# A graph network in one kernel: ranking edges with sums on TensorE, and eight PSUM banks in the convolutions' second product

## The chip, the cores and the metric

The kernel runs on one core of a Trainium2 chip. Its engines work in parallel, each through a list of its own: TensorE (PE) multiplies matrices, VectorE (DVE) and ScalarE (ACT) work element by element, GpSimd (POOL) and the sync engine (SP) mostly start transfers. They wait for each other by semaphores. The metric is the device time of one execution in microseconds; lower is better. PSUM, where PE writes, has eight banks of 512 f32 columns.

## The reference

A graph of 3125 nodes with 256 features and 50,000 edges, sorted by target, passes through four layers. Each adds to x what a graph operation makes of the normalised x:

```python
edge_index = jnp.stack([src, dst])
h = jnp.maximum(_layernorm(x, axis=-1), 0.0)
x = x + _L0_gnn_ref(h, src, dst, ...)      # two attention convolutions, 4 heads
h = jnp.maximum(_layernorm(x, axis=-1), 0.0)
x = x + _L1_gnn_ref(h, edge_index, edge_attr_128, node_vec1, node_vec1_n2, ...)
h = jnp.maximum(_layernorm(x, axis=-1), 0.0)
x = x + _L2_gnn_ref(h, weight, src, dst, edge_type_8, edge_weight)   # relations
h = jnp.maximum(_layernorm(x, axis=-1), 0.0)
x = x + _L3_gnn_ref(h, edge_index, edge_weight, ...)   # two convolutions
```

Two pieces matter here. The second layer sums each edge's 128 attributes over the edge's *source*, while the edges are sorted by target:

```python
sum3d = jax.ops.segment_sum(edge_attr @ W_sum + b_sum, src, num_segments=num_nodes)
cent_term = jax.nn.sigmoid(centralities @ W_cent + b_cent)
vor_term = jax.nn.sigmoid(voronoi_values @ W_vor + b_vor)
```

and the last layer runs this twice:

```python
h = jax.nn.relu(x @ w1 + b1)
agg = jax.ops.segment_sum(ew[:, None] * h[src], dst, num_segments=x.shape[0])
h = agg @ w2 + b2
return jax.nn.relu(_bn(h, g, b))           # statistics over all nodes
```

## The kernel before, in words

Nodes are cut into NT = 25 tiles of 128, edges into two halves of 196 columns of 128. The program has three blocks: one for the setup and the two attention convolutions, one for the middle layers, one for the relations and the last two convolutions (`tail`).

**Sorting the attributes.** In each attention convolution one half of the edge attributes is put in order of the source. DVE works out each edge's place (`rank_half`, one call a half): it marks for every edge and every node tile whether the edge's source lies in that tile (L518), takes running counts over 25 x 196 = 4900 columns (L521), lets PE make prefix sums over the partitions (`rank_prefix`, three small matmuls), adds the tile's offset to the running count and multiplies by the mark, tile by tile (L540, 25 instructions), and sums over the 25 tiles to one place per edge (L543). POOL then writes the rows to their places in DRAM with 196 indirect transfers (the scatters, L509), 128 edges each. SP loads the rows to be scattered into two buffers of seven columns; each is loaded again when its seven scatters are through.

**Setup, engine by engine.** PE makes 25 encoder products, one a node tile: four rows times 512 columns (L1155). Behind the sixteenth, in PE's list, stands the first half's `rank_prefix`. Then come eight transposes of the edges' low index bits (L1164, DVE copies them out at L1133), the projection of the 25 tiles (`pe_project`, L718 and L728, with the second half's `rank_prefix` inside) and the small matmuls for the step tables. ACT takes the sigmoid of each encoder product, POOL adds its two halves and SP stores the sum; in POOL's list the 25 additions stand ahead of the scatters, so the scatters wait for all of them and for the places. DVE does, in order: the first half's places, the edges' integer parts, the eight copies, the row statistics of x (`first_norm`, L565 to L574, in whose middle it waits for ACT's square root), the fold of the attention vectors, the second half's places, the masks (`make_masks`, L807), and the step tables, of which the last instruction is L670.

**The look.** For every edge the scores of its two ends are looked up: 98 groups of four edge columns, in a loop over four groups. A group is 24 matmuls (L910), one-hot vectors from ACT and DVE, a product with the masks (L877) and a sum (L886) on DVE. Softmax follows, then the aggregation. POOL starts the aggregation's gathers (L153) as soon as its scatters are done and the tables are there, and stops after 56 of them, when its ring of 28 slots is full, until the aggregation takes slots out.

**The tail's convolution** (`pe_convolve`, `act_convolve`, `dve_convolve`). The aggregated features, 25 tiles by 256 columns, are turned on PE (two 128x128 transposes a tile, L1606) into one of two PSUM banks, copied out to SBUF a tile at a time, even tiles by ACT and odd ones by DVE (L1615), and multiplied with the second weight in chunks of four tiles (512 columns, L1596) into two other banks, which ACT evicts (L1623) and DVE takes statistics of (L1648). In PE's list the four tiles of the next chunk are turned ahead of the current chunk's product. Four of the eight banks stand idle in this stretch. The batch statistics need all nodes, so all that follows waits for the last chunk.

## Time and profile before

| | us |
|---|---|
| time, median of 3 runs | 4706.84 |
| lowest and highest | 4700.74 and 4716.11 |
| the profiled execution's own time | 4672.72 |
| its span (first to last instruction) | 4671.0 |
| PE busy | 2342.8 (50%) |
| POOL busy | 2384.8 (51%) |
| DVE busy | 2088.9 (45%) |
| ACT busy | 1410.8 (30%) |
| mean granted TensorE clock | 0.711 |

No engine is busy much over half the time, so the shares don't say what bounds the kernel: the stages have different limits, and the timeline of each stage has to be read. The granted clock is a share of 2.4 GHz; in the records PE runs at either 1.2 or 2.4 GHz. A matmul of f32 appears in the trace as two records.

### The profile page before, as it was taken

The numbers are of one execution on the slowest core, as the hardware profiler recorded it, in microseconds if no ns is written. First come the engines' busy times: TensorE is split into PE (matmuls) and PEld (weight loads), VectorE is DVE, ScalarE is ACT, GpSimd is POOL, SyncE is SP. The second block draws the span as 40 slices with busy tenths as digits, with TensorE's granted clock in tenths as the row PEclk, the third lists the DMA queues.
The fourth block names the chain that finished last, engine by engine and source line by source line (L and its number), as shares of the span: only waits on it lengthen the run. The fifth ranks groups of instructions, "written<-read, shape, count | busy, mean of one in ns | idle before, by whom it ended". The sixth has DMA issues, their size and how long they took to land. (4 is left out here: it accounts for less than half of the span.)

```text
span 4671.0 us, 63853 instructions
## 1 busy us (share of the span) xinstructions
PE 2342.8 (50%) x11271; PEld 1694.6 (36%) x11272; DVE 2088.9 (45%) x5444; ACT 1410.8 (30%) x4653; POOL 2384.8 (51%) x2446
## 2 busy tenths in 40 slices
PE   5301646566441246465655834555635556445556
PEld 2201534444330135344444313333423334234334
DVE  6501984445340169654445813333423334233336
ACT  2100746666540146466666710000200001200002
POOL 4775005556637520355552555666366663566660
PEclk9655977777665579677777966666756668666667
DMA  3443433333224334333332842333233331323331
GB/s 111 124 108 91 128 112 91 100 104 104 79 71 119 109 111 127 93 102 101 104 89 74 257 154 83 91 91 92 72 90 91 91 91 37 98 85 91 91 91 40
DMA packets 339578, 465.58 MB, mean 100 GB/s; under 512 B 108191, under 2 KB 253928, under 8 KB 336112
## 3 DMA queue, kind: packets, MB, share of 16 engines
q0 software_dynamic: 113824, 289.70, 21.6%
q1 hardware_dynamic: 157536, 109.12, 8.2%
q10 hardware_dynamic: 67956, 64.45, 4.9%
q14 instruction: 242, 1.98, 0.1%
q8 instruction: 20, 0.33, 0.0%
HBM read 385.88 MB, written 76.97 MB: 99 GB/s over the span
## 5 line engine op out<-in xcount | busy, mean ns | idle before, releaser
L301 PE MATMUL t_ps<-t_ring,t_hot 128*128 x2640 | 884.3, 499 | 893.9 <-DVE t_hot L212 447.7
L153 POOL DMA_INDIRECT ring<-feat_d,srcC x784 | 755.2, 963 | 1060.6 <-ACTq L167 821.2
L301 PEld LDWEIGHTS t_ps<-t_ring,t_hot 128*128 128x128 f32 x2640 | 637.9, 252 | 1140.8 <-issue 1028.7
L153 POOL DMA_INDIRECT t_ring<-feat_d,srcC x784 | 742.2, 947 | 488.0 <-issue 217.6
L175 ACT ACTIVATE ring<-ring,exC 128x64 f32<-128x64 f32 x3136 | 813.4, 336 | 112.1 <-issue 111.0
L301 PE MATMUL bank<-ring,arena 128*128 x1760 | 642.5, 500 | 96.0 <-ACT ring L175 42.9
L910 PE MATMUL wide<-arena 128*128 128x100 bf16 x4704 | 276.9, 217 | 462.7 <-issue 289.4
L509 POOL DMA_INDIRECT attr_d<-abuf,attr_pos x392 | 405.3, 1034 | 191.2 <-issue 129.2
L228 DVE TENSOR_TENSOR acc<-acc,t_ps 128x256 f32 x440 | 184.3, 419 | 712.5 <-DMA arena<-in_L_gnn_ar 223.7
L153 POOL DMA_INDIRECT t_ring<-rel_d,relC x392 | 371.2, 947 | 221.2 <-issue 113.0
L301 PEld LDWEIGHTS bank<-ring,arena 128*128 128x128 f32 x1760 | 400.4, 252 | 174.4 <-issue 120.2
L212 DVE TENSOR_SCALAR t_hot<-lane,dlocT,weightT 128x128 f32<-128x128 f32 x1320 | 412.9, 358 | 94.9 <-issue 63.0
L291 PE MATMUL wide<-arena 128*128 x880 | 243.2, 368 | 410.1 <-DVE arena L220 289.8
L910 PEld LDWEIGHTS wide<-arena 128*128 128x128 bf16 x4704 | 239.8, 102 | 500.2 <-issue 307.7
L291 PEld LDWEIGHTS wide<-arena 128*128 128x128 f32 x880 | 207.3, 255 | 519.7 <-issue 486.3
L1615 ACT COPY t_ring<-t_pt 128x256 f32<-128x256 f32 x26 | 9.6, 369 | 1192.7 <-PE t_pt L1606 1192.7
L877 DVE TENSOR_TENSOR arena<-wide,masks 128x800 f32<-128x800 f32 x196 | 191.9, 979 | 324.7 <-remote 228.8
L228 DVE TENSOR_TENSOR acc<-acc,bank 128x261 f32 x440 | 187.7, 427 | 216.4 <-issue 110.2
L228 DVE TENSOR_TENSOR X<-X,t_ps 128x256 f32 x220 | 92.0, 418 | 348.6 <-DMA X<-in_x 213.7
L206 DVE TENSOR_TENSOR arena<-lane,dlocT 128x256 f32<-128x256 f32 x440 | 185.4, 421 | 121.3 <-issue 107.5
L829 ACT ACTIVATE arena<-arena,ones 128x512 bf16<-128x512 bf16 x196 | 141.4, 722 | 304.7 <-remote 219.9
L234 DVE TENSOR_TENSOR acc_a<-acc_a,wide 128x129 f32 x440 | 127.5, 290 | 200.2 <-issue 129.2
(274 smaller groups left out, 2246.9 us busy)
## 6 DMA issues: line engine op xcount, KB each, us to landing
arena<-lo_d ACTq DMA_DIRECT2D x392, 128.0 KB
rel_d<-mid_stage SPq DMA_DIRECT2D x25, 1024.0 KB
arena<-attr_d SPq DMA_DIRECT2D x98, 260.0 KB
abuf<-in_attr SPq DMA_DIRECT2D x56, 448.0 KB
ring<-feat_d,srcC POOLq DMA_INDIRECT x784
t_ring<-feat_d,srcC POOLq DMA_INDIRECT x784
feat_d<-arena ACTq DMA_DIRECT2D x50, 128.0 KB
feat_d<-t_stage SPq DMA_DIRECT2D x50, 128.0 KB, 1.7
```

Source lines behind the costliest of these rows:

```text
L153: pool.indirect_dma_start(out=ring[:, u % RING, j, 0:D], out_offset=None, in_=table, in_offset=bass.IndirectOffsetOnAxis(ap=index[:, u, j: ...
L175: last = act.activation(part_of_row, part_of_row, ACT.Copy, scale=exC[:, bass.ds(u, 1), j, h])
L206: last = dve.tensor_tensor(hot[:, k % NHOT, :, :], lane[:, :].unsqueeze(1).to_broadcast([P, 2, P]), dlocT[:, bass.ds(s, 1), :].rearrange(" ...
L212: last = dve.tensor_scalar(hot[:, k % NHOT, j, :], lane[:, :], dlocT[:, bass.ds(s, 1), j], weightT[:, bass.ds(s, 1), j], ALU.is_equal, ALU ...
L228: dve.tensor_tensor(acc[:, tile, 0:g.width], acc[:, tile, 0:g.width], ps[k % NHOT][:, 0:g.width], ALU.add).then_inc(g.added, 1)
L234: dve.tensor_tensor(acc_a[:, tile, :], acc_a[:, tile, :], ps_a[k % NHOT][:, 0:AW - 1], ALU.add).then_inc(g.attr_added, 1)
L291: pe.matmul(ps_a[k % NHOT][:, 0:AW - 1], hot_a[:, k % NHOT, :], aring[:, slot, 0:AW - 1], start=True, stop=True).then_inc(g.attr_done, 1)
L301: last = pe.matmul(ps[k % NHOT][:, 0:g.width], hot[:, k % NHOT, j, :], ring[:, slot, j, 0:g.width], start=(j == 0), stop=(j == 1))
L509: pool.indirect_dma_start(out=attr_d, in_=abuf[:, g % 2, k, :], in_offset=None, out_offset=bass.IndirectOffsetOnAxis(ap=attr_pos[:, at + k ...
L829: act.activation(looked[:, k % 2, 1, :], apart[:, k % 2, :], ACT.Relu, scale=-1.0, bias=ones[:, 0:1]).then_inc(s_dst_hot[l], 1)
L877: dve.tensor_tensor(cand[:, k % 2, :, :, :], pk[k % 2][:, :, :].rearrange("p b (s x) -> p (b s) x", x=P)[:, :, 0:HEADS * NT] .rearrange("p ...
L910: last = pe.matmul(pk[k % 2][:, j // 2, at:at + HEADS * NT], looked[:, k % 2, q, j * P:(j + 1) * P], tab[:, piece, q * HEADS * NT:(q + 1) ...
```

## The change

Setup:

- PE's first `rank_prefix` moves ahead of the encoder products. 
- `rank_half` loses its sum over the tiles (L543). The 25 tile products are instead summed by 25 matmuls with the identity into one PSUM bank, `sum_places`. For the first half two of them stand ahead of each encoder product, until all are done ahead of the thirteenth; for the second half all 25 follow the projection.
- The conversion of the sums to places becomes a function of its own, `place_half`. DVE does the row statistics ahead of it in the first half, and the masks ahead of it in the second.
- The eight transposes stand behind encoder product 18, and wait for the first half's places, since both use the same bank. The fold of the attention vectors stands ahead of the wait for the square roots, which is now `first_roots`.
- The sigmoid results have six buffers instead of three. SP loads the attribute groups 2 and 3 ahead of the stores of the low bits.

Tail: tiles are turned in pairs, four transposes into one full bank, over four banks, and copied out a pair at a time; the chunk products use four banks too. The evictions and statistics of chunk r-2 stand ahead of the copies of chunk r's pairs.

```diff
+    NSIG = 6
+    p_pos = wide[0][:, 0, 0:HC]
...
         for n in range(NT):
             dve.scalar_tensor_tensor(out=running[:, n, :], in0=running[:, n, :], scalar=offset[:, n:n + 1],
-                                     in1=mk[:, n, :], op0=ALU.add, op1=ALU.mult)
-        dve.drain()
-        dve.reduce_sum(pos[:, :], running.rearrange("p n j -> p j n"), AX.X)
-        dve.drain()
-        dve.tensor_copy(pos_i[:, 0, :], pos[:, :])
+                                     in1=mk[:, n, :], op0=ALU.add, op1=ALU.mult).then_inc(s_placed, 1)
+        dve.drain()
+
+    def place_half(dve, h):
+        at = h * HC
+        dve.wait_ge(s_ranked, h + 1)
+        dve.tensor_copy(pos_i[:, 0, :], p_pos)
...
+    def sum_places(pe, h, first, last):
+        for n in range(first, min(last, NT)):
+            pe.wait_ge(s_placed, NT * h + n + 1)
+            done = pe.matmul(p_pos, ident[:, :], running[:, n, :], start=(n == 0), stop=(n == NT - 1))
+            if n == NT - 1:
+                done.then_inc(s_ranked, 1)
...
         @block.sync
+            for g in range(2, 4):
+                stage_attr(sp, g)
             for q in range(2):
                 for c in range(4):
                     sp.wait_ge(s_loc, 4 * q + c + 1)
                     sp.dma_start(lo_d[q, c * QC:(c + 1) * QC, :], loT[0:QC, 4 * q + c, :]).then_inc(s_low, 16)
-            sp_weights(sp, 0, 2)
+            sp_weights(sp, 0, 4)
...
         @block.vector
+            first_norm(dve)
+            place_half(dve, 0)
             for n in range(8):
                 dve.wait_ge(s_lot, n + 1)
                 dve.tensor_copy(loT[0:QC, n, :], p_lo[n % 2][0:QC, 0:P]).then_inc(s_loc, 1)
-            first_norm(dve)
             fold_attention(dve, 0)
+            first_roots(dve)
             rank_half(dve, 1)
+            make_masks(dve)
+            place_half(dve, 1)
             dve.sem_inc(s_acol, 1)
-            make_masks(dve)
             step_tables(dve)
...
         @block.tensor
+            pe.wait_ge(s_ready, 1)
+            rank_prefix(pe, 0)
             pe.wait_ge(s_enc_in, 16 * 8)
             for n in range(NT):
+                sum_places(pe, 0, 2 * n, 2 * n + 2)
                 wait_from(pe, s_sig, n - 1)
                 pe.matmul(banks[n % 2][:, :], enc_l[:, n * P:(n + 1) * P], enc_r, start=True, stop=True)\
                   .then_inc(s_enc, 1)
-                if n == 15:
-                    pe.wait_ge(s_ready, 1)
-                    rank_prefix(pe, 0)
+                if n == 18:
+                    pe.wait_ge(s_int, 1)
+                    pe.wait_ge(s_pos, 1)
...
             pe_project(pe, 0)
+            pe.wait_ge(s_loc, 8)
+            sum_places(pe, 1, 0, NT)
...
         def pe_convolve(pe, z):
+            def turn_pair(q):
+                a0, a1 = PAIR[q]
+                if q >= 4:
+                    pe.wait_ge((s_ata, s_atd)[q % 2][z], (q - 4) // 2 + 1)
+                for n in range(a0, a1):
+                    for c in range(KD):
+                        at = c * 2 * P + (n - a0) * P
+                        last = pe.transpose(p_turn[q % 4][:, at:at + P], acc[:, n, c * P:(c + 1) * P], ident[:, :])
+                last.then_inc(s_at[z], 1)
             def chunk(r):
-                    if r:
-                        pe.wait_ge(s_g[z], KD * (r - 1) + c + 1)
+                    if r >= 2:
+                        pe.wait_ge(s_g[z], KD * (r - 2) + c + 1)
                     for a in range(KD):
-                        last = pe.matmul(pf[c][:, 0:(a1 - a0) * P], W2[:, z, a, c * P:(c + 1) * P],
+                        last = pe.matmul(p_proj[(KD * r + c) % 4][:, 0:(a1 - a0) * P], W2[:, z, a, c * P:(c + 1) * P],
                                          AT[:, a, a0 * P:a1 * P], start=(a == 0), stop=(a == KD - 1))
+            for r in range(NR + 1):
+                for q in range(2 * r, min(2 * r + 2, NQ)):
+                    turn_pair(q)
                 if r:
                     chunk(r - 1)
...
         def act_convolve(act, z):
+            for r in range(NR + 1):
+                if r >= 2:
+                    evict(r - 2)
+                if 2 * r < NQ:
+                    copy_turned(act, act.copy, z, 2 * r)
```

PE's list from the start of the setup, before (`wide` are the banks of the ranking and of the low bits, `ring` holds the running counts, `masks` the encoder's input; L1155 is the encoder product, L557 to L559 the prefix sums, L1164 the transposes, L718 the projection's turn):

```order
L1155 MATMUL bank<-masks 128x512 x16
L557 MATMUL wide<-total,before 128x25
L558 MATMUL wide<-total,ones 128x25
L559 MATMUL wide<-ones,total 25x1
L1155 MATMUL bank<-masks 128x512 x9
L1164 MATMUL wide<-ident,exC 98x128 x8
L718 MATMUL bank<-ident,arena 128x128 x4
```

The same stretch of PE's list in the changed kernel (L569 is the sum of the places, L1177 the encoder product, L1185 the transposes; the dots stand for ten more rounds of the two):

```order
L562 MATMUL wide<-total,before 128x25
L563 MATMUL wide<-total,ones 128x25
L564 MATMUL wide<-ones,total 25x1
L569 MATMUL wide<-ring,ident 128x196 x2
L1177 MATMUL bank<-masks 128x512
...
L569 MATMUL wide<-ring,ident 128x196
L1177 MATMUL bank<-masks 128x512 x7
L1185 MATMUL wide<-ident,exC 98x128 x8
L1177 MATMUL bank<-masks 128x512 x6
L732 MATMUL bank<-ident,arena 128x128 x4
```

The prefix sums moved from behind sixteen encoder products to the front, 25 sums came in between the first thirteen, and the transposes moved ahead of the last six.

DVE's list from the first half's tile products on, before:

```order
L540 SCALAR_TENSOR_TENSOR ring<-ring,offset 128x196 x25
L543 TENSOR_REDUCE masks<-ring 128x196
...
L552 SCALAR_TENSOR_TENSOR attr_pos<-masks 128x196
...
L1133 CAST ring<-wide 98x128 x8
L565 BN_STATS stats<-ring 128x6 x25
...
L518 TENSOR_TENSOR ring<-tile_no,hi_f 128x4900
```

The same of the changed kernel:

```order
L543 SCALAR_TENSOR_TENSOR ring<-ring,offset 128x196 x25
...
L577 BN_STATS stats<-ring 128x6 x25
...
L557 SCALAR_TENSOR_TENSOR attr_pos<-ring 128x196
L1151 CAST ring<-wide 98x128 x8
...
L521 TENSOR_TENSOR ring<-tile_no,hi_f 128x4900
```

The reduction is gone, and the row statistics stand ahead of the places.

PE's list in a tail convolution, before, with the bank numbers (L1606 is the turn of a tile, L1596 the product):

```order
L1596 MATMUL t_pf0<-t_ring,t_w2 128x512 x2
L1596 MATMUL t_pf1<-t_ring,t_w2 128x512 x2
L1606 MATMUL t_pt0<-ident,acc 128x128 x2
L1606 MATMUL t_pt1<-ident,acc 128x128 x2
L1606 MATMUL t_pt0<-ident,acc 128x128 x2
L1606 MATMUL t_pt1<-ident,acc 128x128 x2
```

The same of the changed kernel (L1620 the turn, L1631 the product):

```order
L1631 MATMUL t_pf0<-t_ring,t_w2 128x512 x2
L1631 MATMUL t_pf1<-t_ring,t_w2 128x512 x2
L1620 MATMUL t_pt0<-ident,acc 128x128 x4
L1620 MATMUL t_pt1<-ident,acc 128x128 x4
L1631 MATMUL t_ps2<-t_ring,t_w2 128x512 x2
L1631 MATMUL t_ps3<-t_ring,t_w2 128x512 x2
L1620 MATMUL t_ps0<-ident,acc 128x128 x4
L1620 MATMUL t_ps1<-ident,acc 128x128 x4
```

A bank of the turns now comes back after four pairs instead of after one other tile.

## Rows read from the trace of the kernel before

**Rows 1.** Timeline of DVE, setup: start us, duration us, engine, line, operation, [idle before].

```profile
55.87 0.15 DVE L528 COPY col_f<-wide 25x1 f32<-25x1 f32 x1 [32.08 <-PE wide L559]
57.00 11.35 DVE L540 SCALAR_TENSOR_TENSOR ring<-ring,offset 128x196 f32<-128x196 f32 x25
68.42 8.83 DVE L543 TENSOR_REDUCE masks<-ring 128x196 f32<-128x4900 f32 x1
...
85.76 8.25 DVE L565 BATCH_NORM_STATS2 stats<-ring 128x6 f32<-128x256 f32 x25
...
103.21 5.26 DVE L518 TENSOR_TENSOR ring<-tile_no,hi_f 128x4900 bf16<-128x4900 f32 x1 [0.75 <-issue]
108.55 10.37 DVE L521 TENSOR_TENSOR_SCAN ring<-ones,ring 128x4900 f32<-128x4900 f32 x1
...
187.71 0.62 DVE L670 CAST relC<-bank 128x196 int32<-128x196 f32 x2
```

**Rows 2.** Timeline of PE, setup.

```profile
27.01 27.67 PE L1155 MATMUL bank<-masks 4*128 4x512 f32 x32 [27.01 <-DMA masks<-in_L_gnn_b_vor]
...
80.42 0.66 PE L1164 MATMUL wide<-ident,exC 128*98 128x128 f32 x2 [8.93 <-DVE exC L1121]
...
84.85 0.66 PE L1164 MATMUL wide<-ident,exC 128*98 128x128 f32 x2 [0.17 <-DVE ring L1133]
...
104.33 2.13 PE L728 MATMUL bank<-arena 128*128 128x264 f32 x4
...
109.61 1.15 PE L728 MATMUL bank<-arena 128*128 128x264 f32 x4
```

**Rows 3.** Timeline of POOL, setup.

```profile
72.20 0.73 POOL L1069 TENSOR_TENSOR arena<-arena 128x256 f32<-128x256 f32 x1 [0.98 <-ACT arena L1088]
80.05 1.35 POOL L509 DMA_INDIRECT attr_d<-abuf,attr_pos  x1 [7.13 <-issue]
...
109.62 10.07 POOL L509 DMA_INDIRECT attr_d<-abuf,attr_pos  x1 [0.30 <-issue]
...
355.66 0.97 POOL L509 DMA_INDIRECT attr_d<-abuf,attr_pos  x1 [0.30 <-issue]
...
426.15 0.95 POOL L153 DMA_INDIRECT ring<-feat_d,srcC  x1 [0.30 <-issue]
```

**Rows 4.** Timeline of DVE, first look.

```profile
370.65 0.99 DVE L877 TENSOR_TENSOR arena<-wide,masks 128x800 f32<-128x800 f32 x1 [65.15 <-remote]
...
436.45 0.99 DVE L877 TENSOR_TENSOR arena<-wide,masks 128x800 f32<-128x800 f32 x1 [63.66 <-remote]
```

**Rows 5.** Timeline of PE, first look, then the second layer's.

```profile
416.73 0.24 PE L910 MATMUL wide<-arena 128*128 128x100 bf16 x1 [2.56 <-issue]
...
453.13 0.91 PE L910 MATMUL wide<-arena 128*128 128x100 bf16 x9 [0.46 <-issue]
...
1680.59 1.16 PE L910 MATMUL wide<-arena 128*128 128x100 bf16 x12 [0.46 <-issue]
```

**Rows 6.** Timeline of POOL, second layer's look: its last gather before it waits.

```profile
1671.27 0.95 POOL L153 DMA_INDIRECT ring<-feat_d,srcC  x1 [0.30 <-issue]
```

**Rows 7.** Windows: stretch, length, busy of PE, PEld, DVE, ACT, POOL (xcount), clock, DMA.

```profile
250.00:300.00 50.00, 2.90 (x12) 1.16 (x11) 0.00 (x0) 0.00 (x0) 36.98 (x39) 0.50 0.43 106
...
500.00:600.00 100.00, 61.00 (x1163) 54.84 (x1164) 100.00 (x146) 70.27 (x98) 0.00 (x0) 0.98 0.46 128
```

**Rows 8.** Timeline of PE, first tail convolution.

```profile
3930.02 0.66 PE L1606 MATMUL t_pt<-ident,acc 128*128 128x128 f32 x4 [1.04 <-DVE acc L228]
...
3933.38 3.60 PE L1596 MATMUL t_pf<-t_ring,t_w 128*128 128x512 f32 x8
...
3939.08 3.60 PE L1596 MATMUL t_pf<-t_ring,t_w 128*128 128x512 f32 x8
...
3959.63 0.38 PE L1606 MATMUL t_pt<-ident,acc 128*128 128x128 f32 x2
...
3964.22 0.71 PE L1596 MATMUL t_pf<-t_ring,t_w 128*128 128x128 f32 x4 [0.33 <-ACT t_ring L1623]
```

85 lines of the change are left out of this document (37 added, 48 removed).

## The prediction

> **What bounds the kernel now.** I first read busy time in slices: no engine is full, so the question is asked stage by stage. The changed stages are the setup (first 190 us) and the two tail convolutions (35 us each). For each I read the timelines of PE, DVE and POOL side by side, then the windows further on, to see what the stage hands over.
>
> In the setup DVE has the longest list: it waits 32.08 us for the prefix sums, which stand behind sixteen encoder products on PE [rows 1, 2], and its last table instruction ends at 188.3 [rows 1]. The natural reading is that a shorter DVE list shortens the kernel. The look that follows says otherwise. While POOL issues indirect transfers one behind the other, the look crawls: from 250 to 300 us PE gets through 12 matmul records and DVE through none; from 500 to 600 DVE does 146 instructions, three a group, so a group takes 2.05 us [rows 7]. In the crawl a group takes 436.45 - 370.65 = 65.8 us [rows 4]. POOL's last gather ends at 427.1 [rows 3], and from 453.1 PE runs at full pace [rows 5]. The second layer repeats it: last gather ends at 1672.2 [rows 6], full pace from 1680.6 [rows 5]. So nearly all of the 98 groups wait for POOL to stop, and setup time is passed on only through that moment. Whatever slows PE there (the rows call its gaps "issue") I take as found.
>
> POOL's stop is its scatters' start plus a block of fixed length: 80.05 to 427.1, 347 us for 196 scatters and 56 gathers [rows 3]. The tables (188.3) are ready 168 us before the gathers need them (scatters end at 356.6). And the start waits for two things: the last encoder addition, which ended at 72.93, and the places, which came 7.1 us later [rows 3]. After the change I must ask which is late.
>
> In the tail convolution PE is the bound: a chunk begins every 5.70 us (3933.38, then 3939.08), of which 8 product records take about 3.4 us (3.60 with the last one's latency) and the rest is four turned tiles with waits for the copies out of two banks [rows 8].
>
> **The encoder stretch, part by part.** Prefix sums first: they are out about 25 us, as soon as DVE's totals are (it stops at 23.8 = 55.87 - 32.08), so the 25 tile products start about 26.5 instead of 57.0 and, at their 11.35 us, end about 38 [rows 1]. The integer parts and the row statistics (8.25 us and some 4 of small work) follow and end about 54; they now fill what was a wait. DVE's 8.83 us sum is gone twice.
>
> On PE the first half gains 25 sums. No row shows a 128x128 by 196-column f32 product, so I bound it by the nearest: four records of 264 columns took 2.13 us at the low level, thus 1.07 a product, times 196/264 = 0.79 us; at the high level 1.15, thus 0.43 [rows 2]. Less than nothing is excluded, since PE has to do them. The encoder products take 27.67/16 = 1.73 us each [rows 2]. That is the low clock: 0.865 a record of 512 columns, where the tail's records of that size take 0.43 to 0.45 (3.60/8) [rows 8]. I take 0.72 a sum, between its scaling from the 264-column row and from the encoder's record (0.865 x 196/512 x 2 = 0.66): 18 us. The eight transposes with their copies (80.42 to 85.5, [rows 2]) now stand inside the encoder's list, and add about 4.7 us. So the products end at 27.0 + 25 x 1.73 + 18 + 4.7 = 93 us, where they ended about 71.4, and the last addition 1.5 us later, at 94.5. The places are ready long before: the sums end at 27.5 + 12 x 1.73 + 18 = 66.3 and DVE's five small steps take 2.8 (77.25 to 80.05, [rows 1, 3]): 69. What is late next is the encoder: the scatters start at 94.3, **14 us later** than before. Behind the additions on POOL's list stand just these scatters. ACT's square root too waits behind the last sigmoid (about 93.5); DVE's second half starts near 96 instead of 103.2.
>
> **The rest of the setup.** The second half loses its 8.83 us sum (25 sums on PE lie beside the masks), so the tables end about 7 + 9 = 16 us earlier, at 172. No gather waits for them, so this is worth only an earlier first group of the look; a quarter of a group, 0.5 us. More sigmoid buffers: worth nothing, since ACT waited for PE, not for the stores. SP's attribute loads ahead of the low-bit stores: each waits for seven scatters, which delays the stores to about 130, and the look wants them at 175; nothing. POOL's block stays 347 us: its long issue of 10.07 us lies under DVE's 10.37 us scan [rows 1, 3], and the second half's mark and scan still fall within the scatters (96 to 112). The Trainium skill, "SBUF - State Buffer", section on the "DVE blocks DMA" trap, says that GpSimd can't write descriptors while certain DVE instructions hold the shared port. By that rule the hold goes where the scan goes; the trace agrees (10.07 beside 10.37), and had the scatters started first at 112 the block would be about 19 us shorter.
>
> **When the look gets free.** POOL stops at 427.1 + 14 = 441. The lag to full pace was 26.0 us in the first look and 8.4 in the second [rows 3, 5, 6]. I read the difference as position in the 65.8 us group: the first stop fell into the gap between two groups (PE's last crawling matmul at 416.73 [rows 5], the group ended by 436.45 [rows 4]), in which nothing could speed up; the second fell behind a group's beginning. After the change the group boundaries lie 16 us earlier (354.6, 420.4) and the stop at 441, in the middle of a group's matmuls, so I expect 12 us of lag, from between 8.4 and 26: full pace at 453, which is where it was, with as many groups done. **Setup: 14 later, 14 less lag: 0**, with -4 and +12 as the lag's ends.
>
> **The tail.** The chunk stays 3.43 us; a turned tile back to back costs 0.22 us (3959.63 to the product of the next chunk, whose two records end it in 0.22 to 0.38 [rows 8]), so four cost 0.9 and a period is 4.33 instead of 5.70: 1.37 saved in each of the four full periods, 5.5 us. At the start 16 records with waits took 3.36 us (3930.02 to 3933.38); back to back, and the last pair's copy, 2.0: 1.35 saved. At the end the last chunk waited 0.33 us for an eviction; now it doesn't. Sum 7.2 us a convolution, **14.4 for two**. Cover: ACT per period then has two evictions and a 512-column copy, about 2.0 us, DVE the same, beside 4.33 on PE; a pair is copied one whole chunk before it is needed. If the turns cost twice that (the bounds are 0.22 and 0.38 a tile) the saving is 5 a convolution. The batch statistics wait for the last chunk, so all of it reaches the end.
>
> **Sum.** Profiled execution 4672.7, less 14.4, plus 0: 4658. It stands 34 us below the median of the runs; carried over to that: 4706.8 - 14.4 = **4692 us**. About 0.3%, 14 us, is what a measurement here can tell from none, so this forecast lies on the edge of it.
>
> **Rivals.**
> 1. *The lag stays 26 us* wherever the stop falls. For: it may belong to the first look, not to the position. Against: 8.4 in the other. Then the 14 us late start counts in full: 4692 + 14 = 4706.
> 2. *The sums lift PE's clock.* The encoder products alone ran 45 us at the low level with PE full [rows 2]; the sums are 128-row products like those behind which it rose after 104. With sums and products high the thirteen rounds take 13 x 0.87 + 25 x 0.36 = 20 us, twelve lone products again 1.73: scatters from 76, 4 us earlier than before, and the lag short: setup -20, total 4672. Against: the sums fill less than half of the stretch. The Trainium skill, "TensorE: Matmul & The Clock Gate", Part 1, has the gate opened by sustained busy time; by that alone the encoder stretch would have run high already, which the trace contradicts (1.73 us, not 0.87). By the page it would come out as this rival, or better.
> 3. *Slower: the stop falls into the head of the gap between two groups.* The gap is about 20 us (416.73 to 437, [rows 4, 5]); behind it PE needed 16 more. If the boundaries don't shift as I think and the stop comes at the gap's start, the lag is 36: setup +14 +10 = +24, total 4692 + 24 = 4716, slower than before. It decides from a lag of 27 us on.
> 4. *The look isn't held by POOL's stop*, and DVE's 16 us come through: 4692 - 16 = 4676. Against: rows 7. For: only that I can't name what slows PE.
>
> **Chances.** Forecast 0.40, rival 1 0.20, rival 2 0.13, rival 3 0.15, rival 4 0.08; the remaining 0.04 is something unseen. The forecast's cloud (4685 to 4700) is split between faster and same. Faster 0.24 + 0.02 + 0.13 + 0.08 = 0.47, slower 0.09 of rival 3 plus 0.03 and 0.02 of the rest = 0.14, same 0.39. Range 4668 (rival 2) to 4720 (rival 3); the forecast's own is 4684 to 4704.
>
> **What the changed profile would show.** Encoder products in rounds of about 3.2 us and the last addition near 94; scatters from 94 (76 in rival 2). Product records of 0.43 us in that stretch would refute the low clock. Last gather at 441, tables at 172, the lag read between them and the first full-pace group, of 12 (26 in rival 1, 36 in rival 3). In the tail, chunks every 4.33 us and 27.7 us from first turn to last eviction. The forecast is wrong if scatters don't start later, or if the look reaches full pace before POOL stops.

## The result

| | before | after |
|---|---|---|
| median of 20 runs, us | 4706.84 | 4715.72 |
| lowest and highest | 4690.56 to 4721.62 | 4706.78 to 4726.79 |
| the profiled execution's own time | 4672.72 | 4715.71 |
| its span | 4671.0 | 4713.2 |

The ratio is 1.0018, 95% interval 1.0010 to 1.0027: the change makes the kernel slower by 5 to 13 us. The forecast was 4692 us, with 0.47 on faster, 0.39 on the same and 0.14 on slower. The two profiled executions differ by 43 us, the medians by 9: the profiled execution of before was 34 us shorter than its median, and shorter than every one of its twenty runs. So differences are read here stage by stage, and not from the spans.

### The profile page after: what moved, and what is told of

Same layout as the page of the kernel before. It is cut to its first block and busy times, and to the rows that moved or that the text cites. A ratio compares the mean times of both kernels' runs of the same rounds, so it can differ in the third digit from the quotient of the medians.

```text
span 4713.2 us, 64027 instructions
## 1 busy us (share of the span) xinstructions
PE 2379.8 (50%) x11371; PEld 1726.8 (37%) x11372; DVE 2065.1 (44%) x5430; ACT 1410.2 (30%) x4641; POOL 2398.7 (51%) x2446
## 5 line engine op out<-in xcount | busy, mean ns | idle before, releaser
L301 PE MATMUL t_ps<-t_ring,t_hot 128*128 x2640 | 888.2, 502 | 902.1 <-DVE t_hot L212 456.1
L220 DVE TENSOR_SCALAR arena<-lane,arena,minus_tile 128x128 f32<-128x128 f32 x440 | 159.1, 362 | 145.1 <-issue 81.8
```

The source lines that it names most:

```text
L220: dve.tensor_scalar(hot_a[:, k % NHOT, :], lane[:, :], aring[:, slot, AW - 1:AW], minus_tile[:, g.attr, bass.ds(s, 1)], ALU.subtract, ALU. ...
L301: last = pe.matmul(ps[k % NHOT][:, 0:g.width], hot[:, k % NHOT, j, :], ring[:, slot, j, 0:g.width], start=(j == 0), stop=(j == 1))
```

## The profile after

The page of the changed kernel, its first rows:

```profile
span 4713.2 us, 64027 instructions
PE 2379.8 (50%) x11371; PEld 1726.8 (37%) x11372; DVE 2065.1 (44%) x5430; ACT 1410.2 (30%) x4641; POOL 2398.7 (51%) x2446
```

PE's timeline in the setup answers to [rows 2] (start, duration, engine, line, operation, idle before and its releaser):

```profile
23.53 0.59 PE L562 MATMUL wide<-total,before 128*128 128x25 f32 x2 [23.53 <-DVE offset L529]
...
28.04 2.07 PE L1177 MATMUL bank<-masks 4*128 4x512 f32 x2
30.04 1.68 PE L569 MATMUL wide<-ring,ident 128*128 128x196 f32 x4
31.64 2.07 PE L1177 MATMUL bank<-masks 4*128 4x512 f32 x2
...
70.66 12.31 PE L1177 MATMUL bank<-masks 4*128 4x512 f32 x14
82.90 0.67 PE L1185 MATMUL wide<-ident,exC 128*98 128x128 f32 x2
...
86.01 10.60 PE L1177 MATMUL bank<-masks 4*128 4x512 f32 x12
```

A round of two sums and a product takes 31.64 - 28.04 = 3.60 us. Behind the last sum a product takes 1.76 again (12.31/7), and the eight transposes with their copies 3.1 (82.90 to 86.01). The list ends at 96.6.

POOL's timeline answers to [rows 3]: the last addition, the first scatter, and the last gather before its wait.

```profile
97.32 0.72 POOL L1085 TENSOR_TENSOR arena<-arena 128x256 f32<-128x256 f32 x1 [0.98 <-ACT arena L1104]
98.22 1.16 POOL L512 DMA_INDIRECT attr_d<-abuf,attr_pos  x1 [0.17 <-issue]
...
446.37 0.95 POOL L153 DMA_INDIRECT ring<-feat_d,srcC  x1 [0.30 <-issue]
```

The first scatter is 18.2 us later than before (80.05), and POOL stops at 447.3 instead of 427.1, so its block is 349.1 us long, 347 before.

DVE's timeline of the first look, answering to [rows 4]: one product with the masks a group.

```profile
365.61 0.99 DVE L891 TENSOR_TENSOR arena<-wide,masks 128x800 f32<-128x800 f32 x1 [65.30 <-issue]
432.33 0.99 DVE L891 TENSOR_TENSOR arena<-wide,masks 128x800 f32<-128x800 f32 x1 [64.58 <-remote]
473.80 0.99 DVE L891 TENSOR_TENSOR arena<-wide,masks 128x800 f32<-128x800 f32 x1 [39.19 <-PE wide L924]
475.86 0.98 DVE L891 TENSOR_TENSOR arena<-wide,masks 128x800 f32<-128x800 f32 x1
```

Full pace begins at 473.80, 26.5 us behind POOL's stop. In the kernel before, the same count gave 453.48 - 427.1 = 26.4. So the look, too, is 20 us later, and ends at 666.0 instead of 645.6.

PE's timeline of the first tail convolution, answering to [rows 8]:

```profile
3983.30 1.09 PE L1620 MATMUL t_pt<-ident,acc 128*128 128x128 f32 x8 [0.65 <-DVE acc L228]
...
3989.65 3.60 PE L1631 MATMUL t_ps<-t_ring,t_w 128*128 128x512 f32 x8
3993.09 1.04 PE L1620 MATMUL t_ps<-ident,acc 128*128 128x128 f32 x8
3993.96 3.60 PE L1631 MATMUL t_pf<-t_ring,t_w 128*128 128x512 f32 x8
...
4009.67 1.05 PE L1631 MATMUL t_pf<-t_ring,t_w 128*128 128x128 f32 x8
```

A chunk every 4.31 us (5.70 before), and 27.4 us from the first turn to the end of the last product record (34.9 before); the second convolution is the same, 27.4.

Between these stages the two profiles drift further apart: the changed kernel is 20 us behind at the first look's full pace, 30 at the second's (1710.83 against 1680.88, by DVE's products) and 53 at the tail's first turn (3983.30 against 3930.02). Most of that lies in the execution of before, not in the change: from the second look's full pace to the first turn it took 2249 us, where the five profiled kernels with the new tail (the changed one and four of the experiments, on chips on which before takes about 4705 us) took 2266 to 2278.

Setup +20, tail -15: this already names the direction. The experiments had to show whether these two do add up, why the encoder's list became so long, and what the first scatter's time is worth.

## The experiments

They fell on several chips, and this turned out to matter. On four of them the kernel before takes 3535 to 3537 us, on one 4703, like the chip of the forecast. Every run is compared with the kernel before on its own chip. I call the four the A chips, and that one and the forecast's the B chips (in the expectations the two are "conditions"). One window tells them apart, 250 to 300 us, in the first look (busy time and count of each engine, granted clock, DMA share, GB/s), first the changed kernel on the B chip:

```profile
250.00:300.00 50.00, 2.95 (x17) 1.46 (x17) 1.84 (x3) 0.72 (x1) 36.90 (x39) 0.50 0.43 106
```

and the setup-only kernel on an A chip:

```profile
250.00:300.00 50.00, 30.91 (x576) 27.76 (x576) 50.00 (x72) 34.31 (x49) 33.24 (x35) 0.97 0.83 217
```

POOL issues its scatters at much the same pace (39 and 35), but on the A chip PE does 576 matmul records beside them, on the B chip 17. There the crawl doesn't exist, and the look takes 2.1 us a group from its first.

**1. The two halves of the change.** `setup_only` is the changed kernel with the tail functions of before; `tail_only` the reverse. Edit: the change's own hunks, all of the setup or all of the tail.

> The change's setup alone, with the tail of before. Theory T (the setup counts only through the moment at which POOL stops issuing its scatters and gathers, and that moment goes by the encoder's last addition plus a fixed block of 347 to 349 us): first scatter at about 98, stop at about 447, the look at full pace at about 475, the two convolutions at 34.9 us each as in before; +20 us, so a ratio of 1.004 (4727 against 4707). Rival A (the setup costs nothing that the median shows, and the stages behind it are slower by themselves): first scatter at 98 too, but a ratio of 1.000 to 1.002. Rival B (the whole of the +9 us comes from the tail's code): ratio of 1.000.

> The change's tail alone, with the setup of before. Theory T: first scatter at 80, stop at 427, look at full pace at 453, each convolution 27.4 us instead of 34.9; -15 us, a ratio of 0.9968. Rival A (the stages behind the setup are slower by themselves): -15 us too, and the setup-only kernel tells. Rival B (the eight banks cost more elsewhere than they give): ratio of 1.000 or more.

Measured, both on an A chip: setup_only 1.0057 (1.0043 to 1.0071), +20 us; tail_only 0.9957 (0.9943 to 0.9971), -16 by the medians. The sum is +4. Rivals A and B fall. The halves were not run by themselves on a B chip. But the reason I gave for the setup can't be right on this chip, where no look waits for POOL's stop. What takes its place is seen in POOL's waits. On the A chip (setup_only, from 395 to 900 us; line waited for, us in total, times, longest):

```profile
POOL ring L153 <- issue: 107.6, 353, 0.3
POOL ring L153 <- ACTq L167: 11.6, 38, 0.3
```

and on the B chip (the changed kernel, 447 to 1290 us):

```profile
POOL ring L153 <- ACTq L167: 425.1, 71, 268.2
```

On the A chip POOL never waits for a free slot of the first layer's ring longer than 0.3 us. From its first scatter to the end of the next layer's scatters it goes through its list with short waits only: 26 of them, 35 us in all, are for the rows that SP loads (3.1 us at most), and none of any kind is over 4.4 us. So its own list is the bound there, and a delay of its first scatter is passed on one for one; that this holds for the total too is what the table behind the experiments tests. (The chain of waits on that page can't show it: the 31% that POOL has in it are all gathers of later layers, into `t_ring`.)

On the B chip the same 19 us come through another gate, POOL's stop and the look behind it. I call the joint form T2: what counts of the setup is the first scatter.

**2. The sums on DVE again.** `prefix_reduce` keeps the early prefix sums, the six buffers and the new tail. DVE sums over the tiles again, and converts the first half's sums to places right behind them, ahead of the integer parts and the row statistics.

```
 in rank_half / place_half:
-            ... .then_inc(s_placed, 1)
+        dve.reduce_sum(pos, running.rearrange("p n j -> p j n"), AX.X)
 on PE:
-                sum_places(pe, 0, 2 * n, 2 * n + 2)
-                if n == 18: (the eight transposes)
+            (the eight transposes behind the encoder's loop)
-            sum_places(pe, 1, 0, NT)
```

> The changed kernel, but the sums over the 25 tiles go back to DVE as one reduction, right behind the tile products, and the transposes go back behind the encoder products; the prefix sums stay first, the sigmoids keep six buffers, the tail is the changed one. Theory T with the PE list as the cause of the late additions: the encoder products stand at 2.0 to 2.2 us each again, the last addition at 72 to 80, first scatter at 72 to 80, stop at 419 to 427, full pace at 445 to 453; with the tail's -15 us the ratio to before is 0.995 to 0.997. Rival (position theory: the lag from POOL's stop to full pace depends on where in a group of the look the stop falls): the same stop, but full pace off by up to 14 us either way. Rival (the six buffers or POOL and ACT themselves make the additions late, not PE's list): first scatter stays at 95 or later, ratio 1.002.

Measured: 0.9942 (0.9928 to 0.9955), and on another A chip (below, `prefix_again`) 0.9923 (0.9910 to 0.9937), both under the 0.995 to 0.997 that I expected, which was reckoned for a B chip. First scatter at 71.8, as expected. The encoder on PE is one row now:

```profile
27.16 43.03 PE L1177 MATMUL bank<-masks 4*128 4x512 f32 x50 [2.02 <-DMA masks<-in_L_gnn_b_vor]
```

25 products in 43.0 us, 1.72 each, and DVE, which has nothing to wait for, has the places at 46.4. PE's list made the additions late, not the six buffers, which this kernel has too.

**3. Gathers behind the look.** Edit: `pool.wait_ge(s_sum[l], LOOKS + 2)` ahead of each layer's gathers.

> The changed kernel with one more wait in each attention layer: POOL starts its first 56 gathers when the look is over, instead of right behind the scatters. Theory T (the look crawls at 65 us a group of four edge columns while POOL issues indirect transfers back to back, and reaches 2.05 us a group some 25 us after it stops): layer 1 stops at 374 instead of 447, full pace at about 400 instead of 475, look over at about 590 instead of 666; in layer 2 the look starts at full pace from its first group, some 60 us earlier; the gathers then fit into the softmax, which takes 49 us; in all -110 to -140 us against the changed kernel, ratio to before about 0.972. Rival (the crawl comes from something else that ends at 450 to 475, such as the transfers' landing, the clock, or the scores' table): full pace stays at 450 to 475 and the gathers behind the look add 20 to 70 us to each layer, ratio 1.01 to 1.03. Rival (the aggregation now starts late, since its first slots are filled only in the softmax, and softmax crawls while POOL issues): the look gains as T says but the softmax grows by as much, ratio 1.00.

> The kernel gathers_wait once more, for the condition in which before takes about 4705 us. There, theory T (POOL's back-to-back indirect transfers make the look crawl, and it reaches full pace 26 us after they end): scatters over at 374, nothing behind them until the look is done; full pace at 400 instead of 474, look over at 592 instead of 666, in layer 2 the look at full pace from its first groups; -110 to -150 us against the changed kernel, ratio to before 0.970 to 0.980. Rival (the look's pace depends on something else that ends at 450 to 475): full pace at 450 to 475, ratio 1.01 or more. Rival (the gain of the look is given back by gathers that now fall into the softmax and slow it): look over at 592, aggregation no more than 20 us earlier, ratio 0.995 to 1.002. In the other condition (before at 3535): as measured, 1.009.

> As for gathers_wait_again: with before at about 4705, theory T has full pace at 400, the look over at 592 and -110 to -150 us against the changed kernel (ratio to before 0.970 to 0.980); the rival with another cause of the crawl has full pace at 450 to 475 and a ratio of 1.01 or more; the rival in which the gathers' crawl moves into the softmax has the look over at 592 and a ratio of 0.995 to 1.002. With before at about 3535: 1.009 as measured twice.

Measured on three A chips: 1.0093, 1.0096 and 1.0079 (intervals within 1.0058 to 1.0112). There the scatters end at 393.7 and the look at 389.2, so the first layer has no wait, while in the second POOL stands from 1172.4 to 1206.7, 34 us. POOL's list being the bound, most of that comes out: 26 or 27 us against the changed kernel. It was made to tell whether the look of a B chip is released by the end of the scatters or by the stop of POOL, but it never ran on one. So that POOL's transfers hold the look there stays a reading of the timelines, and no run shows it by removing them.

**4. The changed kernel on an A chip, and its transposes and sums moved.** `transposes_late` puts the eight transposes behind the encoder's loop again; `sums_behind` the 25 sums too, ahead of them.

```
 sums_behind:
             for n in range(NT):
-                sum_places(pe, 0, 2 * n, 2 * n + 2)
                 ... (the encoder product)
+            sum_places(pe, 0, 0, NT)
+            (the eight transposes)
```

> The changed kernel, unchanged. In the four kernels run so far the kernel before took 3535 us, not 4707, and its look ran at 2.1 us a group from the start instead of 65; POOL waited nearly nowhere. Theory T2 (in this condition POOL's list of scatters and gathers is the bound from its first scatter on, so that every us by which the first scatter moves comes out at the end, one for one): first scatter at 98 to 99 against 80, +19 to +20, the tail -15; ratio 1.0010 to 1.0020. Rival (the effects of setup, +20, and tail, -15, don't add up): a ratio under 1.000 or over 1.003. Should this run meet the other condition (before at about 4707): 1.0018, the profile as seen before.

> The changed kernel with the eight transposes of the low bits back behind the last encoder product; the places' sums stay between the products. Theory T2: PE's encoder list gets 3 us shorter, the last addition goes from 97 to 94, first scatter at 95, -3 us at the end against the changed kernel (ratio to before about 1.0005). Rival (the transposes stood in a gap of PE's and cost nothing): first scatter stays at 98.

> The changed kernel with all 25 sums of the first half's places behind the last encoder product (and the transposes behind them). Theory T2: the products stand at 1.71 us each, the last one ends at 70, the additions at 72; then 25 sums of 0.8 us (no product between them) end at 90, and the places are there at 92 to 93; first scatter at 93, -5 to -6 us against the changed kernel (ratio about 0.9998). Rival (the sums are dear only between products, for the clock or for the bank): the sums take 0.4 us each when they stand alone, first scatter at 82 to 83, ratio about 0.997. Rival (a wait that is not PE's): first scatter stays at 98.

Measured: after_again 1.0020 (1.0011 to 1.0029), first scatter at 98.1; transposes_late 1.0012 (1.0002 to 1.0023), at 95.6; sums_behind 0.9976 (0.9965 to 0.9988), at 83.7. The change has the same price on both kinds of chip, 1.0018 and 1.0020. Without the transposes in PE's list the first scatter comes 2.5 us earlier, and the medians differ by 2 us (3 expected). The sums alone were not 0.8 us each, as I expected, but as the rival had it, 0.44:

```profile
70.01 11.08 PE L569 MATMUL wide<-ring,ident 128*128 128x196 f32 x50
```

The windows of these records alone (66 to 81 us) show why; the first column behind the length is PE's busy time and count.

```profile
66.00:70.00 4.00, 0.00 (x0) 0.00 (x0) 1.00 0.18 66
70.00:74.00 4.00, 3.99 (x12) 3.99 (x13) 1.00 0.18 66
74.00:78.00 4.00, 4.00 (x22) 4.00 (x22) 1.00 0.01 4
78.00:81.00 3.00, 3.00 (x19) 2.79 (x17) 1.00 0.00 0
```

Twelve records in 4 us are 0.33 each, the pace of 1.2 GHz; nineteen in 3 us are 0.16, that of 2.4. (The granted clock's column reads 1.00 in all of these, also where a record has the length of 1.2 GHz, so I go by the durations here.) Behind 43 us of four-row products PE stood at the low level; 128-row products in a row lifted it, and mixed with four-row ones, as in the changed kernel, they didn't. So 26.5 us of longer list (96.6 against 70.1) are 11.1 for the sums by themselves, 3.1 for the transposes, and 12 for mixing the sums with the products; 9 of the 12 are the sums (0.80 us each instead of 0.44) and 3 to 4 the products between them (2.00 instead of 1.72).

**5. Two other mixtures.** `sums_first` has the 25 sums ahead of the encoder's loop; `five_a_round` has `sum_places(pe, 0, 5 * n, 5 * n + 5)` in it.

> The changed kernel with all 25 sums of the first half's places ahead of the first encoder product (the transposes stay behind product 18). Theory T2 with the pace of PE as it was seen: sums at 26.4 to about 37 (they follow DVE's tile products, which end at 34.7), then products at 0.865 us a record again although the sums stood before them, the last at 83, first scatter at 84 to 85, so -13 to -14 us against the changed kernel, ratio to before about 0.998. Rival (128-row sums bring PE to its high pace and the four-row products keep it): products at 0.43 us a record, additions limited by ACT and POOL, first scatter at 62 to 68, ratio 0.992 to 0.994. Rival (it is only the amount of PE's work, not the alternation, that counts): the list ends at 96, first scatter stays at 98, ratio 1.002.

> The changed kernel with five sums ahead of each of the first five encoder products instead of two ahead of each of the first thirteen; nothing else is moved. A round of two sums and a product took 3.60 us: 1.71 for the product as it stands alone, 2 x 0.67 for the sums at PE's low pace, and 0.55 that is left for the change from one to the other. Theory T2 with a price per change: 8 rounds fewer, -4.4 us, first scatter at 93 to 94, ratio 1.0007. Rival (the extra is per sum): first scatter stays at 98, ratio 1.002. Rival (five sums in a row, 2 to 3 us, are enough to raise PE's pace): sums at 0.33 to 0.44 us, first scatter at 88 to 91, ratio 0.999 to 1.000.

Both ran on the B chip. Measured: sums_first 0.9973 (0.9958 to 0.9989), first scatter at 82.0; five_a_round 0.9976 (0.9958 to 0.9995), at 81.6. PE's rows in five_a_round:

```profile
27.03 3.63 PE L569 MATMUL wide<-ring,ident 128*128 128x196 f32 x10 [1.90 <-DMA masks<-in_L_gnn_b_vor]
30.60 2.07 PE L1177 MATMUL bank<-masks 4*128 4x512 f32 x2
...
37.44 1.93 PE L569 MATMUL wide<-ring,ident 128*128 128x196 f32 x10
39.30 1.12 PE L1177 MATMUL bank<-masks 4*128 4x512 f32 x2
...
45.13 21.25 PE L1177 MATMUL bank<-masks 4*128 4x512 f32 x30
```

My price per change of kind (0.55 us) is refuted: the first scatter comes 12 us earlier than that gave. The third rival was nearer (88 to 91 for the 81.6 measured): from the third round on five sums take 1.93 us, not 3.63, and the product between them 1.12, not 2.07; both at the high level. sums_first came out 2 to 3 us earlier than expected (84 to 85), since its products don't fall to the low level at once. The products' own windows, first just behind the sums, then further on:

```profile
37.40:41.00 3.60, 3.60 (x8) 1.23 (x9) 1.00 0.05 16
41.00:66.00 25.00, 25.00 (x31) 9.12 (x30) 0.51 0.24 87
```

Eight records of 0.45 us, then 0.81 at a granted clock of 0.51, which is 1.2 GHz: the four-row products don't keep the level that the sums won. The Trainium skill, "TensorE: Matmul & The Clock Gate", Part 1, ties the level to how busy PE has been. The trace doesn't agree with that alone: PE was full from 41 to 66 and fell, and full before 70 in sums_behind and didn't rise. What differed was the kind of product, four rows or 128. The number of columns doesn't explain it: the tail's products have 512 columns as well, but 128 rows, and run at 0.43 us a record (3.60/8 with the end of the last one).

**6. The additions on DVE.** `adds_dve` is prefix_reduce with POOL's 25 additions put into DVE's list, among the places, integer parts and row statistics. Two things had to move with them: SP loads three groups of attributes amid and right behind the stores of the encoder's sums, and DVE folds the attention vectors ahead of its eight copies. `first_and_dve` in addition takes the first half's places from PE, with the sums ahead of the encoder.

```
-            for n in range(NT):                       (POOL)
-                pool.wait_ge(s_sig, n + 1)
-                pool.tensor_tensor(sigb[...], ..., ALU.add).then_inc(s_term, 1)
+    def add_halves(dve, first, last):                 (DVE, called from seven places of its list)
+        for n in range(first, last):
+            dve.wait_ge(s_sig, n + 1)
+            dve.tensor_tensor(sigb[...], ..., ALU.add).then_inc(s_term, 1)
```

> prefix_reduce with the 25 additions of the encoder's halves on DVE, between its other work, instead of on POOL, so that POOL's first scatter waits for the places alone; two loads of scatter groups are issued amid the stores of the encoder's sums. Theory T2: places and first scatter at 46 to 48 instead of 71.8, scatters over at about 340, 56 gathers at about 412; DVE's list is 8 us longer, so look, softmax and the start of the aggregation's additions come 6 to 10 us later, at 429 to 433, and POOL, which has filled its ring, now waits for them: of the 25 us only 2 to 8 come out at the end, ratio about 0.992 to 0.994. Rival (POOL's list is the bound whatever comes: all 25 us come out): ratio 0.987. Rival (the look's later start costs more than the scatters' earlier one gives): ratio 0.995 or more. Should the run meet the other condition (before at 4707): stop of POOL at 412 instead of 419 to 427 and more, the look at full pace some 25 us after it, ratio 0.992.

> adds_dve once more. With before at about 4705: first scatter at 47.8, stop at 398 to 399, full pace at 424, so 32 us earlier than before, and the tail's 15: ratio 0.990, which is 0.001 above first_and_dve's 0.9887 in that condition, since there POOL's block alone counts. With before at about 3535: 0.988 as measured, under first_and_dve's 0.989.

> adds_dve with the first half's places summed on PE ahead of the encoder instead of by DVE's reduction: first scatter at 39 to 41 instead of 47.8. The encoder's products start 10 us later, so look, softmax and the aggregation's first addition come 8 to 12 us later, at 434 to 438. Theory T2 with its limit (POOL's list is the bound only as long as the aggregation starts by the time at which POOL's 56 gathers are through, which adds_dve reached with a first wait of 6.7 us): no gain, +2 to +10 us against adds_dve, ratio 0.988 to 0.991. Rival (POOL's list alone counts): -8 us, ratio 0.9855.

> first_and_dve once more, for the condition in which before takes about 3535 us. There, T2 with its limit: first scatter at 41 against 47.8 of adds_dve, but the aggregation's first addition at 434 to 438 against 426, POOL waits for it 10 to 20 us, total not under adds_dve's: ratio 0.988 to 0.991. Rival (POOL's list alone counts): 0.986. In the other condition (before at 4705): as measured, 0.989.

Measured on A chips: adds_dve 0.9877 (0.9856 to 0.9899) and 0.9860 (0.9839 to 0.9881), first_and_dve 0.9891 (0.9876 to 0.9906); on the B chip first_and_dve 0.9887 (0.9867 to 0.9908). With adds_dve I had counted on POOL's waiting for a later look and on 2 to 8 of 25 us to come out (0.992 to 0.994). The first scatter came 24 us earlier, and 21 and 23 us of that came out, as the rival had it. Its longest wait was this:

```profile
418.88 0.95 POOL L153 DMA_INDIRECT ring<-feat_d,srcC  x1 [0.30 <-issue]
426.49 0.94 POOL L153 DMA_INDIRECT ring<-feat_d,srcC  x1 [6.67 <-ACTq L167]
```

The look began at 170.7, not later than prefix_reduce's 169.1, and the aggregation's first addition came at 426.3, 3 us later instead of 6 to 10. One step on, the limit is there; first_and_dve, whose first scatter stands at 40.4:

```profile
405.77 1.55 POOL L153 DMA_INDIRECT ring<-feat_d,srcC  x1 [0.30 <-issue]
432.27 0.95 POOL L153 DMA_INDIRECT ring<-feat_d,srcC  x1 [24.95 <-ACTq L167]
```

POOL has filled its ring at 407.3 and stands for 25 us until the aggregation starts. The 7 us by which its scatters start earlier are lost, and the kernel takes 9 to 12 us more than adds_dve. On A chips adds_dve is the fastest kernel of this study, 1.2 to 1.4% under the one before. It did not run on a B chip, so whether it or first_and_dve is faster there is open.

**7. More work ahead of the look.** `masks_twice` is prefix_reduce with `make_masks(dve)` a second time, some 22 us more on DVE and nothing on POOL; `prefix_again` is its partner.

> prefix_reduce with the masks made twice on DVE, 22 us more of DVE's work ahead of the look and none on POOL's list. Theory T2 with its limit: first scatter stays at 72, the look and the aggregation's first addition come 22 us later, at 445; POOL's 56 gathers are through at about 437, so 8 to 14 us of the 22 come out, ratio 0.9965 to 0.998. Rival (only POOL's first scatter counts): ratio 0.994. Rival (the look is the bound after all): all 22 us come out, ratio 1.0005.

> masks_twice once more, for the condition in which before takes about 3535 us. There, T2 with its limit: first scatter at 72, the aggregation's first addition at 445 against 423 of prefix_reduce, of the 22 us 8 to 14 come out: ratio 0.9965 to 0.998 (prefix_reduce: 0.9942). Rival (only the first scatter counts): 0.994. Rival (the look is the bound): 1.0005. In the other condition (before at 4705): equal to prefix_again within 0.15%, since the 22 us lie ahead of a look that crawls until POOL's stop.

> prefix_reduce once more, as the partner of masks_twice. In the condition with before at 4705: first scatter at 72, stop at 422 to 424, full pace at 448 to 450, ratio 0.995 to 0.996. In the other (before at 3535): as measured, 0.994.

Measured on one A chip: masks_twice 0.9945 (0.9932 to 0.9959), prefix_again 0.9923 (0.9910 to 0.9937). The first scatter is the same (71.3 and 71.9) and the aggregation's first addition comes at 447.7 against 423.2, yet only 6 us come out, under the 8 to 14 expected; POOL's longest wait for a slot was 2.3 us. On the B chip masks_twice has 0.9954 (0.9938 to 0.9970), by T2 from its first scatter 0.9950: there the 22 us cost nothing that can be measured. So DVE's list ahead of the look is covered on the B chip, and nearly so on an A chip, and with it goes the worth of the 13 us by which the change has the tables ready earlier (175.7 against 188.3).

## All of it against the first scatter

By T2 a kernel's difference to before is the shift of its first scatter, from 80.1 us, less 15.2 for the new tail (tail_only's ratio: 0.0043 of 3535). The measured column is the difference of the medians on the same chip; by the intervals it is good to 3 to 8 us on A chips and 4 to 10 on B chips.

| kernel | first scatter | by T2 | measured |
|---|---|---|---|
| setup_only, A (old tail) | 99.5 | +19 | +20 |
| after_again, A | 98.1 | +3 | +6 |
| transposes_late, A | 95.6 | 0 | +4 |
| sums_behind, A | 83.7 | -12 | -9 |
| prefix_reduce, A, twice | 71.8 | -24 | -22, -27 |
| masks_twice, A | 71.3 | -24 | -21 (look 24 us later) |
| adds_dve, A, twice | 47.8 | -48 | -45, -48 |
| first_and_dve, A | 40.4 | -55 | -36 (POOL waits 25) |
| after, B | 98.2 | +3 | +9 |
| sums_first, B | 82.0 | -13 | -16 |
| five_a_round, B | 81.6 | -14 | -16 |
| masks_twice, B | 71.9 | -23 | -20 |
| first_and_dve, B | 41.3 | -54 | -57 |

Over 50 us of shift the line holds within 6 us on both kinds of chip; on A chips it ends where POOL's ring is full before the aggregation starts. The changed kernel lies 3 us above it on the A chip and 6 on the B chip. Both are just beyond its own intervals, but the 15.2 for the tail is itself known to 5 us only; whether there is anything to explain is open.

The lag from POOL's stop to the look's full pace, on B chips, against how far the stop lay in a 65 us group:

| kernel | POOL's stop | DVE's last product before it | between them | first at 2.05 us a group | lag |
|---|---|---|---|---|---|
| five_a_round | 430.2 | 419.5 | 11 | 456.1 | 25.9 |
| after | 447.3 | 432.3 | 15 | 473.8 | 26.5 |
| sums_first | 431.6 | 415.9 | 16 | 458.0 | 26.5 |
| masks_twice | 423.6 | 368.3 | 55 | 449.7 | 26.2 |
| before | 427.1 | 370.7 | 56 | 453.5 | 26.4 |
| first_and_dve | 391.8 | 331.9 | 60 | 415.3 | 23.4 |

(The product is the one with the masks, one a group.) The lag is 26 us in five kernels and 23 in the sixth, with the stop anywhere from 11 to 60 us behind the last product.

## Why the prediction was wrong

**The step that failed is the lag.** "So I expect 12 us of lag, from between 8.4 and 26." It rested on reading the difference of 26.0 and 8.4 as position in the group. The forecast wanted 12 us for a stop in the middle of a group's matmuls; the changed kernel's stop falls there, 15 us behind the last product, and its lag is 26.5. The table above has positions from 11 to 60 us, and lags of 23 to 26.5. The group boundaries were wrong as well: not 16 us earlier than before (354.6 and 420.4) but 4 to 5 (365.6 and 432.3). The 8.4 comes back in the second layer, where the changed kernel has it again:

```profile
1701.09 0.96 POOL L153 DMA_INDIRECT ring<-feat_d,srcC  x1 [0.30 <-issue]
```

```profile
1710.49 1.41 PE L924 MATMUL wide<-arena 128*128 128x100 bf16 x15 [1.19 <-issue]
```

1702.0 to 1710.5. By DVE's products the second layer's lag is 8.6 to 9.2 us in all six kernels. But there the stop always falls within 4 us of a group's product (in before 3.3 us behind it, in the changed kernel 0.9 ahead of it), a position that no first look of the table has. So these runs don't tell whether the short lag comes from the layer or from that position, and what makes the first look's lag three times as long wasn't found. One thing it isn't: transfers still under way. From 450 to 470 us the changed kernel moves nothing (the last two columns are the DMA share and GB/s), and PE still does only 8 matmul records in these 20 us:

```profile
450.00:470.00 20.00, 1.95 (x8) 0.82 (x8) 0.00 (x0) 0.00 (x0) 0.00 (x0) 0.50 0.00 0
```

With 14 us later and 14 less lag the forecast's setup came to nothing; without the second it stands at its full price. This was rival 1 (4706, chance 0.20); the result lies 9 us above even that, in part because of the next two points. Of the 23 us between forecast and result, 14 are the lag, 4 the scatters' start and 2 POOL's block; 3 are left over.

**The encoder stretch was mis-sized by 4 us.** Forecast: last addition at 94.5, scatters from 94.3; measured 98.0 and 98.2. The sums were taken at 0.72 and took 0.80; the products were taken at 1.73 and took 2.00 as long as sums stood between them, which no row of before could show; the transposes were taken at 4.7 and took 3.1. (The forecast's two times also contradict each other: the scatters, at 94.3, can't start ahead of the last addition's end, at 94.5.) The direction of this step, later scatters from a change that shortens DVE's list, was right, and it is what the whole result hangs on.

**POOL's block** was nearly right: 349 us for 347. So was the tables' being worth nothing: their last instruction ended at 175.7 (forecast 172, before 188.3), and masks_twice shows that 22 us more ahead of the look cost nothing measurable on the B chip and 6 us on an A chip.

**The tail** was right: 4.31 us a chunk for 4.33, 27.4 us for 27.7 (both to the end of the last product; the forecast calls it the last eviction), 15 us for 14.4, and alone, on an A chip, 0.9957.

**The rivals.** Rival 2, the sums lift the clock, is false for this change (product records of 1.04 us between sums) and partly true for others: with five sums a round or all in a row the level rises, and the scatters start 16 us earlier than in the changed kernel, though still 2 us later than before (81.6 and 82.0 against 80.1; the rival had 76). Rival 3 named 4716, which is what was measured, for a wrong reason: its lag of 36 occurs nowhere. Rival 4 says that POOL's stop doesn't hold the look. That is so on the A chips, but what the rival makes of it is wrong: DVE's 16 us don't come through there either, since POOL's list is the bound.

The sum with measured terms: 4706.8 + 18.2 (first scatter) + 2 (block) - 15 = 4712, against 4715.7.

## What to carry to other kernels

Before an engine's long wait is removed, find whose list gates the stage behind it, here POOL's first indirect transfer, and price every instruction that the change puts ahead of that one: the sums on PE saved DVE 9 us twice that nobody waited for, and together with the transposes they made POOL's scatters 18 us later. If an engine's list is the bound, take foreign work off it first; on A chips moving 25 additions from POOL to DVE gave some 22 us more than the early prefix sums and the tail alone. Two lags at two places make no law: without a third point, take the one measured at the place that is forecast.

## What was not expected of the hardware

- The same kernel takes 3535 us on four chips and 4703 on another: there, while POOL issues indirect transfers one behind the other, most of PE's matmuls in the look start 1.4 to 2.8 us apart (17 matmul records in 50 us for 576). This goes on for 23 to 26.5 us in the first look, and about 9 in the second, after POOL has stopped, also while no transfer runs. Why was not found.
- Four-row f32 products of 512 columns stayed at the low level through 43 us of a full PE (0.86 us a record), and went back to it (0.81 a record on the mean, granted clock 0.51) when 128-row sums ahead of them had ended at the high one (0.16 for 196 columns).
- Between 128-row sums at the low level a four-row product took 2.00 us instead of 1.72, and a sum 0.80, where five in a row took 0.71 each ((30.60 - 27.03)/5).
